# Products of constants added to TensorE's queue at five places of a sequence mixer, feed-forward and expert kernel

## The reference

```python
h = rmsnorm(layernorm(x), ln1_w)
zxbcdt = h @ in_proj_w                        # 512 -> 2576 columns
z, xb, B, C, dt = split(zxbcdt)
xBC = silu(causal_depthwise_conv(xb|B|C))     # 4 taps over the rows
y = scan over 16 chunks of 128 rows, 16 heads # exp of cumulated decays, chunk states carried on
y = rmsnorm((y + D*x) * silu(z), norm_w)
h = layernorm(x) + y @ out_proj_w             # residual of the mixer
h = h + silu(h2 @ gate_w) * (h2 @ up_w) @ down_w   # h2 = rmsnorm(h, ln2_w), 2048 wide
x = x + h
x = x + top-2-of-8 experts(layernorm(x))      # router, gather, three products per expert, scatter
```

## Time and profile before

| What | Value |
|---|---|
| median of 3 runs | 1528.81 us |
| profiled execution | 1526.85 us, span 1525.1 us |
| mean granted TensorE clock | 0.985 of full |
| PE busy | 1444.7 us, 95% of the span |
| DVE busy | 775.2 us, 51% |
| ACT busy | 446.2 us, 29% |
| POOL busy | 447.2 us, 29% |
| `project` | 0 to 287 us |
| `ssd` | 287 to 582 us |
| feed-forward | 584 to 1109 us |
| router and experts | 1109 to 1525 us |

### The profile page before, as it was taken

One profiled execution on the slowest core, in us unless ns is written; L12 is line 12 of the kernel. 1 busy time (PEld: TensorE's weight loads), 2 busy tenths in 40 slices (PEclk: granted clock), 3 DMA queues, 4 the chain that ended last, 5 costly groups with the idle time before them and its releaser, 6 DMA issues.

```text
span 1525.1 us, 19801 instructions
## 1 busy us (share of the span) xinstructions
PE 1444.7 (95%) x6871; PEld 1052.3 (69%) x6871; DVE 775.2 (51%) x1235; ACT 446.2 (29%) x926; POOL 447.2 (29%) x497
## 2 busy tenths in 40 slices
PE   6799999889999998999999999999988999999996
PEld 4577778556666666888888888888867555555553
DVE  6969778699999992333333332333465221211211
ACT  4444445455555552212112121211121111111110
POOL 2402121257777662101011010101012233333332
PEclk9999999899999998999999999999999999999998
DMA  9123123622332225010000001200476122222220
GB/s 195 56 104 105 68 83 133 206 90 105 117 119 98 98 71 193 28 28 29 14 28 28 14 28 28 97 7 12 148 244 232 57 77 79 87 87 84 81 64 17
DMA packets 84978, 130.97 MB, mean 86 GB/s; under 512 B 29213, under 2 KB 45597, under 8 KB 84896
## 3 DMA queue, kind: packets, MB, share of 16 engines
q1 hardware_dynamic: 71488, 103.62, 21.0%
q0 software_dynamic: 9360, 25.18, 5.4%
q10 hardware_dynamic: 4048, 1.10, 0.3%
HBM read 91.59 MB, written 43.78 MB: 89 GB/s over the span
## 4 chain that ended last, share of the span: by engine, by line
PE 38%; DMA 15%; issue 4%; DVE 3%; ACT 0%; POOLq 0%; POOL 0%; DVEq 0%; ACTq 0%
PE fin_bank L1744 35%; DMA result_rows<-out_dram,idx 8%; DMA out_dram<-result_rows,idx 7%; DVE result_rows L1729 2%; PE fin_bank L1885 1%; PE fin_bank L1854 1%; PE fin_bank L1867 0%; PE fin_bank L1812 0%; PE fin_bank L1800 0%; DMA xs<-xn_rows,idx 0%; DVE ff_w_lo L1581 0%; PE fin_bank L1903 0%; DVE fi_bn L1616 0%; ACT ff_w_hi L1505 0%; PE fin_bank L1810 0%
## 5 line engine op out<-in xcount | busy, mean ns | idle before, releaser
L1744 PE MATMUL fin_bank<-ff_hT_hi,ff_w_hi 128*128 128x512 f32 x512 | 203.0, 397 | 3.2 <-DVE ff_w_lo L1551 3.2
L1744 PE MATMUL fin_bank<-ff_hT_hi,ff_w_lo 128*128 128x512 f32 x512 | 202.7, 396 | 0.0
L1744 PE MATMUL fin_bank<-ff_hT_lo,ff_w_hi 128*128 128x512 f32 x512 | 202.7, 396 | 0.0
L1885 PE MATMUL fin_bank<-wx,xT 128*128 x624 | 192.9, 462 | 1.0 <-ACT xT L1520 0.8
L1543 DVE TENSOR_TENSOR ff_prod<-ff_prod,fin_bank 128x512 f32<-128x512 f32 x64 | 44.0, 688 | 263.8 <-PE fin_bank L1744 263.8
L1388 POOL TENSOR_TENSOR ff_w_lo<-ff_stage,ff_w_hi 128x1024 fp32r<-128x1024 f32 (+1 forms) x24 | 56.5, 2354 | 411.7 <-ACT ff_w_hi L1495 406.9
L1885 PEld LDWEIGHTS fin_bank<-wx,xT 128*128 128x128 f32 x624 | 116.4, 192 | 60.0 <-issue 2.7
L1729 DVE SCALAR_TENSOR_TENSOR result_rows<-fin_bank,wt,result_rows 128x512 f32<-128x512 f32 x39 | 29.3, 751 | 234.6 <-DMA result_rows<-out_dram,idx 232.1
L628 PE MATMUL pj_bank<-hT_hi,w_in_hi 128*128 128x512 f32 x336 | 135.7, 404 | 11.8 <-DVE zst L548 8.7
L530 DVE SCALAR_TENSOR_TENSOR conv_acc<-raw,conv_w,conv_acc 128x512 f32<-128x512 f32 x144 | 113.2, 786 | 42.6 <-ACT raw L339 35.1
L628 PE MATMUL pj_bank<-hT_lo,w_in_hi 128*128 128x512 f32 x336 | 133.9, 398 | 0.0
(11 more groups left out here) (264 smaller groups left out, 2455.0 us busy)
## 6 DMA issues: line engine op xcount, KB each, us to landing
cv_rows<-cst SPq DMA_DIRECT2D x12, 1024.0 KB, 4.2
cv<-cv_rows SPq DMA_DIRECT2D x16, 768.0 KB, 4.3
zs_rows<-zst SPq DMA_DIRECT2D x8, 1024.0 KB, 6.5
zs<-zs_rows SPq DMA_DIRECT2D x16, 512.0 KB, 5.3
wx<-in_L_ffn_Wg_dram SPq DMA_DIRECT2D x8, 704.0 KB, 8.4
wx<-in_L_ffn_Wu_dram SPq DMA_DIRECT2D x8, 704.0 KB, 9.0
w_raw<-in_L_attn_in_proj_w_dram SPq DMA_DIRECT2D x32, 128.0 KB, 3.8
x<-_attn_hidden_states_dram SPq DMA_DIRECT2D x16, 256.0 KB, 5.6
```

Of the source, the lines that this page charges most:

```text
L1744: mm = eng.matmul(ps, w[a], x[b], start=first and i == 0, stop=last and i == 2)
L1885: mm = eng.matmul(ps[:, 0:EI], xT[j % 2][:, k, :], wx[:, bass.ds(e, 1), at:at + EI].rearrange("p a n -> p (a n)"), start=(k == 0), stop=(k ...
```

## The change

A helper `idle_products(n)` is added to `project`; it issues n products of the constants `ones` and `ident`, 128 columns each, into `turn[1]`. It is called with 28 at the start of the block, with 30 at the start of the second row group (behind the wait for the turned rows), and with 14 behind the last block. In `ssd`, 14 such products stand ahead of the last `turn_h2`, in bank `cb_ps[0]`, behind a wait for the last `score`. In `finish`, 13 stand ahead of the first `width`, in `warm_ps`. No other engine's instructions change.

```diff
+            def idle_products(n):
+
+                for i in range(n):
+                    eng.matmul(turn[1][:, 0:P], ones[:, :], ident[:, :], start=True, stop=True)
+
+            idle_products(28)
             for k in range(KD):
                 turn_rows(0, k)
             for g in range(NGRP):
                 if g:
                     eng.wait_ge(s["hT_lo"], (g + 1) * KD)
+                if g == 1:
+                    idle_products(30)
                 for n, (kind, i) in enumerate(ORDER[g]):
...
                     if g + 1 < NGRP and AT_TURN - 1 <= n < AT_TURN - 1 + KD:
                         turn_rows(g + 1, n - AT_TURN + 1)
+            idle_products(14)
...
                 if late and now:
                     row_sums(e)
+                if f == TILES - 1:
+                    eng.wait_ge(s["score"], 4 * TILES)
+                    for i in range(14):
+                        eng.matmul(cb_ps[0][:, 0:P], ones[:, :], ident[:, :], start=True, stop=True)
                 if later and c != TILES:
                     turn_h2(f)
...
+            for i in range(13):
+                eng.matmul(warm_ps[:, 0:P], ones[:, :], ident[:, :], start=True, stop=True)
             width(0, 0)
```

## The result

The changed kernel takes 1533.07 us (median of 16 runs, 1530.59 to 1537.34) against 1529.14 us (16 runs, 1525.55 to 1532.16) of the kernel before on the same chip: ratio 1.0029, 95% interval 1.0019 to 1.0039, slower by 2.9 to 6.0 us. The forecast was 1533.0 us with a range of 1529.8 to 1535.4. The profiled execution took 1532.64 us (span 1530.9).

A forecast was written before the change was run, and what follows sets the result against it. PE's queue was taken to bound row groups 1 to 3 and the feed-forward. +6.7 + 0 - 2.2 - 0.3 = +4.2 us on the profiled 1526.85 made 1531.05, and 2 us for the median gave 1533.0; range 1529.8 to 1535.4.

The forecast's parts named there:

- 30 products at group 1: Start of row group 1: no wait there, so the products cost 30 x 0.223, +6.7 us; bounds 3.4 and 6.7.
- beginning: Kernel start: 28 products fit while PE is idle, half clock from 20 to 23 us stays; 0, bounds -1.5 and +1.
- passage to the scan: Ahead of the scan's barrier: 14 products are free and the scan starts at full clock; -2.2 us, bounds 0 and -3.8.
- last turn and feed-forward: Passage to the feed-forward: turn 0.5 us faster, 13 products 1.3 us in the way; -0.3 in all, bounds +0.2 and -1.8.
- the second fall: Scan's first chunk: the clock falls again after PE's 2.04 us wait for DVE's decay; expected to stay, earlier.
- the second rival: Both passages: the scan gives all of 3.8 us, the feed-forward 0.3; sum +2.6, 1531.4 us; chance 0.22.
- the clock at 1.00 from 283 to 304 us: Passage to the scan and first chunk: a clock staying full there was named as showing the prediction wrong.
- list of half-clock stretches: Whole kernel: stretches at 1.2 GHz near 20, 283.5 to 304 and 575.8 to 589.7 us, 23.6 us in all.
- the passages give back all: Clock never falls at the passages: 3.8 and 1.8 us come back, perhaps 1.0 at the beginning; +0.1, 1528.9 us; chance 0.12.
- they give nothing: Passages give next to nothing: clock falls again or ACT and DVE stand in for PE; +6.5, 1535.3 us; chance 0.15.
- the 30 products fall into a wait: Row group 1: the 30 products fall into a wait after all; -2.5, 1526.3 us; chance 0.02.
- all the half-clock time comes back: Five places: half of their half-clock time, 11.8 us, all comes back; sum -5.1, 1523.7 us; chance 0.02.

The follow-up runs named there:

- 30 moved, alone: Kernel before plus only 30 products ahead of group 0's 13th block, in PE's wait for DVE's gate step: ratio 0.9995.
- all but group 1: Changed kernel without its 30 products in row group 1, the other four places kept: ratio 0.9984 against the kernel before.
- feed-forward alone: Kernel before plus only the 14 products ahead of the last turn and the 13 ahead of the feed-forward: ratio 1.0004.
- scan alone: Kernel before plus only the 14 products at the projection's end, ahead of the barrier to the scan: ratio 0.9982.
- last turn alone: Kernel before plus only the 14 products ahead of the last turn, none ahead of the feed-forward: ratio 0.9976.
- group 1 alone: Kernel before plus only the 30 products at the start of row group 1: ratio 1.0044.
- the beginning alone: Kernel before plus only the 28 products at the start, run as two copies: ratios 0.9986 and 0.9992.
- the split: Kernel before plus 18 products ahead of the last turn and 6 ahead of the feed-forward: ratio 0.9984.
- the two with the moved products and other places: Changed kernel with its 30 products moved into group 0's wait, with and without the feed-forward's 13: ratios 0.9954 and 0.9961 against the kernel before.
- renamed copy: Kernel before with one more comment line, its instructions the same: ratio 0.9997.

## Why the prediction was right

By place, read from the single profiled executions:

| term | predicted | changed kernel | alone |
|---|---|---|---|
| 30 products at group 1 | +6.7 | +6.62 between the matmuls | +6.63 at the mark |
| beginning | 0 | +0.48 by 64.97 us | -0.38 by 64.11 us, and -0.24 to -0.45 in the five kernels that change only what comes later |
| behind group 0's wait | none | +1.48 | -0.03 to +1.32 with nothing changed up to the wait's end |
| passage to the scan | -2.2 | -3.38 to the first `yg` | -1.94 |
| last turn and feed-forward | -0.3 | -0.26, and -0.25 ahead of it | -0.02 |
| sum | +4.2 | +4.66 at the mark | |

**Row group 1** was right in mechanism and size. The experiments show it twice, by adding the 30 products alone and by taking them alone out.

**The scan** was right in mechanism: the pause shrinks, PE starts at the full clock, and the second fall stays at DVE's `decay`. That is what four of the five kernels with these 14 products show, with 9.53 to 9.66 us from turn to `yg`, 1.9 to 2.1 less than before's 11.60. The changed kernel is the fifth, and in it the step failed: the clock stayed full from 293 to 304.3 us, so it got 3.38 us, nearly the bound of 3.8 that the second rival took. In all 14 kernels this way goes with the time at half clock in it: 8.22 us with none, 9.53 to 9.66 with 3.0 to 3.4 us of it, 11.28 to 11.62 with 6.7 to 8.2, and 12.64 or 12.65 where all of it is at 0.50. Without the scan's products it is therefore 11.28 to 12.65 us, and the -1.94 of the kernel with them alone is counted from one of these values. Had nothing else differed, the sum would have been 4.2 - 1.2 = +3.0. The prediction named "the clock at 1.00 from 283 to 304 us" as a sign against itself, and so it came.

**The wait of group 0** was missing from the prediction. Its 8.75 us lie in the first row group, of which I had looked at the beginning and the end only. The prediction's list of half-clock stretches adds up to 23.6 us, while the mean clock of 0.985 stands for about 46 us (2 x 0.015 x 1525); this stretch, at 0.50 from 60.65 to 67.47 us, was one that the list lacked. Here is what it costs; the moment at which the clock is back is read from the granted clock in stretches of a quarter of a microsecond:

| kernel | wait ends | clock is back | half clock behind the wait | wait's end to turned dt, less the 30 products |
|---|---|---|---|---|
| 30 moved, alone | 64.13 | not down | 0 | 38.42 |
| all but group 1 | 64.86 | 67.69 | 2.83 | 39.68 |
| before | 64.49 | 67.47 | 2.98 | 39.77 |
| feed-forward alone | 64.04 | 68.50 | 4.46 | 40.46 |
| scan alone | 64.06 | 68.89 | 4.83 | 40.60 |
| last turn alone | 64.11 | 69.76 | 5.65 | 41.01 |
| group 1 alone | 64.25 | 69.99 | 5.74 | 41.09 |
| after | 64.97 | 71.08 | 6.11 | 41.25 |

The last column less half of the one before it is 38.2 or 38.3 us wherever the clock was down, and 38.4 where it was not. So the loss of 1.48 us is, within a tenth, half of the 3.13 us more that the clock was down. The kernels with group 1's products or the last turn's alone have nearly the same loss with nothing changed ahead of the place, so no product has to stand ahead of it for this. The two stretches of the kernel with the last turn's products alone:

```profile
64.00:68.00 4.00, 3.89 (x9) 3.12 (x10) 1.47 (x3) 0.00 (x0) 3.57 (x7) 0.50 0.00 0
68.00:72.00 4.00, 4.00 (x15) 3.15 (x15) 3.89 (x7) 0.60 (x1) 0.26 (x2) 0.78 0.00 0
```

So the total came within half a microsecond because two misses, +2.0 (1.48 and the 0.48 by which the wait ended late) and -1.2, nearly cancelled. That was luck. What was right for its reasons is the large term and the sign.

**The feed-forward** was right in mechanism: a gain at the turn (0.66 us for 1.11), products that fall partly at half clock (4.52 us for 26 rows), a first matmul 6.61 us after the turn, where the prediction had 586.4 - 579.8 = 6.6, and a 14th that starts 0.26 us sooner. That the size agrees within 0.1 us is in part luck too, since the same way takes 9.42 to 10.03 us where nothing is changed in it.

**The beginning** was right at most in its size. The changed kernel's turns take the same 3.49 us, but for another reason than before: the products had brought the clock up, and it fell again at 13.06 us, behind the pauses between 10.5 and 13.04 (in the kernel with the beginning alone it fell later, and the turns took 2.84 us). The prediction's word that the products change nothing around 20 us does not hold in general: with them alone the clock was at 0.50 from 14.2 to 20.97 us and not from 19.7 to 23.1. Little of this reaches the end of group 0's wait, which comes at 64.04 to 64.97 us in all kernels. Of the six kernels with the 28 products four reach it at 64.69 to 64.97, later than each of the eight without (64.04 to 64.51), and two at 64.11; whether they cost up to half a microsecond in company is not shown.

The prediction also took from the earlier trace rows that turns alone bring the clock up. The changed kernel supports it: its clock fell at 13.06 and was back at 16.46 us, with nothing but the 14 turns on PE in between. But of the eight kernels without the 28 products only three start the projection at the full clock behind the same turns (0.30 or 0.31 us between its first two matmuls); the other five start it at half (0.56 or 0.57).

**The rivals.** That the passages give back all (+0.1) is out: the kernel with all but group 1 is 1.2 to 3.8 us faster, not 6.6. Its mechanism, a clock that never falls in the scan's first chunk, did come in the changed kernel, and there alone. That they give nothing is out by the same interval, and that the 30 products fall into a wait by the +6.63 us that they cost alone. That all the half-clock time comes back is out too. The scan's chunk had about 8.7 us of it before and the changed kernel none, and half of that, 4.3 us, stands against 3.38 won: PE's wait of 2.05 us for DVE's `decay` stays. The Trainium skill ("TensorE: Matmul & The Clock Gate", "Terms") puts the penalty at about the throttled time times the share of the clock withheld; behind group 0's wait, where PE works without a pause, the runs agree (1.48 us for half of 3.13), in the scan's chunk they give less.

**What stays open.** Why the clock stays down for a shorter or a longer time behind the same wait, which decides up to 1.5 us at either place; whether it stays up in the scan in every execution of the changed kernel, as it did in the profiled one, is not known either. And why the kernels with the beginning's or the last turn's products alone, and the split, have 2.4 to 3.5 us less in their whole times than their marks say (the two with the moved products and other places 2.3 to 3.8): the part behind the mark differs by single executions as much, and no row of it stood out.

## What to carry to other kernels

Products that hold the clock up belong only where the queue of PE stands still anyway, and must end before what it waits for arrives: the same 30 cost 6.6 us between two blocks 0.23 us apart, and gained 1.1 to 1.6 at the mark inside a wait of 8.75. Look for the long waits of PE in the timeline with half-clock work behind them, not for a boundary in the code, and check the list of half-clock stretches against the mean clock of the page. Count the products against the wait (six nearly fit ahead of the feed-forward, thirteen did not). Compare kernels place by place up to a moment of their timelines: a renamed copy repeated to 0.03 us, but an edit elsewhere moved the same moment by 1.3, so a shift of that size counts for a place only when the rows of the place itself show it.

## What the runs showed of the hardware

The profiled executions of two equal programs agree within 0.03 us over 1151 us, while one that differs only at 575 us and later took 1.24 us longer from the end of group 0's wait to the turned dt (41.01 for 39.77), with 5.65 us at the lower clock behind the wait for 2.98. Behind this wait, where PE works without a pause, each microsecond at 1.2 GHz cost half a microsecond, within a tenth of a microsecond in all, in the eleven kernels in which the clock was down. A wait of 2.05 us on DVE in the scan's first chunk saw the clock fall in or behind it in four kernels and not in the fifth, which had the same instructions around it. In the changed kernel the clock came back from 0.50 in a stretch in which PE ran 14 turns and nothing else (13.04 to 16.50 us). A product of constants takes 0.221 us at the full clock in a row (6.62 us for 30), and in the feed-forward's passage, partly at half clock, 4.28 us for 13 (591.29 - 587.01), or 0.33.
